# Gate logits taken from eight extra columns of two other products

## What is computed

```python
x = x + _L0_conv_ref(_gn(x), ...)          # linear attention on group-normed x
t = _to_tokens(x)
t = t + _L1_attn_ref(_ln_t(t), ...)        # softmax attention, 8 heads, + b_agg
t = t + _L1_ffn_ref(_ln_t(t), ...)         # routed experts
# inside the last:  gate_logits = ln(t) @ gate_weight   (256 x 8)
#                   gates = sinkhorn(max(logits, 1e-6)), 8 rounds; top 128 tokens for each of 8 experts
```

## Time and profile before

| what | us |
|---|---|
| median of 3 runs | 1494.82 (1491.95 to 1495.4) |
| span of the profiled execution, first to last instruction | 1467.7 |
| PE, PE weight load, DVE, ACT, POOL busy in it | 1339.3, 915.8, 1021.3, 868.7, 562.6 |
| mean granted TensorE clock, share of full speed | 0.950 |
| length of one ordinary attend (585 to 735 us, and so on) | 150 |

### The profile page before, as it was taken

One profiled execution on the slowest core, in us unless ns is written; L12 is line 12 of the kernel. 1 busy time (PEld: TensorE's weight loads), 2 busy tenths in 40 slices (PEclk: granted clock), 3 DMA queues, 4 the chain that ended last, 5 costly groups with the idle time before them and its releaser, 6 DMA issues.

```text
span 1467.7 us, 29142 instructions
## 1 busy us (share of the span) xinstructions
PE 1339.3 (91%) x10849; PEld 915.8 (62%) x10849; DVE 1021.3 (70%) x2114; ACT 868.7 (59%) x1268; POOL 562.6 (38%) x1068
## 2 busy tenths in 40 slices
PE   5789989999999999999999999999998999987535
PEld 3556656667576767676767676656666567766423
DVE  3536766858585857586768676787789776899771
ACT  2456557677667767677666767665675667542100
POOL 1132530445134513551245214520554116875443
PEclk9899989999999999999999999999999999999665
DMA  2051013600360037002710272005500265454322
GB/s 79 29 137 51 1 30 87 172 16 27 80 184 15 2 93 193 18 2 75 184 46 2 57 168 79 2 30 117 144 15 2 65 169 191 128 158 134 118 68 80
DMA packets 66785, 119.13 MB, mean 81 GB/s; under 512 B 10705, under 2 KB 46546, under 8 KB 66642
## 3 DMA queue, kind: packets, MB, share of 16 engines
q1 hardware_dynamic: 57682, 90.48, 22.9%
q0 software_dynamic: 8960, 26.75, 6.0%
HBM read 29.11 MB, written 33.55 MB: 43 GB/s over the span
## 4 chain that ended last, share of the span: by engine, by line
PE 62%; DVE 24%; issue 6%; POOL 4%; ACT 3%; DMA 0%; DVEq 0%; POOLq 0%; ACTq 0%
PE shared L938 30%; PE scores L894 12%; PE acc L916 11%; DVE prob_sum L1635 6%; PE acc L913 3%; PE shared L933 3%; DVE acc_sb L1609 2%; DVE bn L1344 2%; ACT probs L1209 2%; DVE work L1543 1%; PE acc L926 1%; DVE resid L1350 1%; DVE best_i L1541 1%; DVE best L1539 1%; DVE bn_x L1404 1%
## 5 line engine op out<-in xcount | busy, mean ns | idle before, releaser
L1209 ACT ACTIVATE probs<-scores 128x1024 f32<-128x1024 f32 x512 | 516.0, 1024 | 178.1 <-PE scores L894 94.0
L894 PE MATMUL scores<-query_stack,key_stack 96*128 96x256 f32 x2048 | 342.1, 308 | 16.0 <-ACT probs L1209 15.7
L1635 DVE TENSOR_TENSOR prob_sum<-prob_sum,probs 128x512 f32<-128x512 f32 x512 | 331.3, 707 | 0.0
L894 PEld LDWEIGHTS scores<-query_stack,key_stack 96*128 96x128 f32 x2048 | 275.9, 192 | 85.1 <-issue 39.1
L916 PE MATMUL acc<-probs,v_all 128*32 128x256 f32 x4096 | 289.2, 389 | 0.0
L1242 POOL TENSOR_TENSOR attn_T<-acc_sb 128x256 f32<-128x256 f32 x56 | 41.4, 740 | 447.8 <-DVE acc_sb L1609 445.0
L938 PE MATMUL shared<-w_sb,chan 128*128 128x512 f32 (+1 forms) x512 | 186.7, 501 | 5.9 <-DVE chan L1438 5.9
L916 PEld LDWEIGHTS acc<-probs,v_all 128*32 128x32 f32 x4096 | 114.8, 110 | 104.0 <-issue 37.9
L938 PEld LDWEIGHTS shared<-w_sb,chan 128*128 128x128 f32 x512 | 91.9, 192 | 62.5 <-issue 57.9
L938 PE MATMUL shared<-chan,w1T 128*128 128x512 f32 x256 | 121.3, 608 | 2.1 <-ACT chan L1125 2.1
L1635 DVE TENSOR_TENSOR prob_sum<-probs 128x512 f32<-128x512 f32 x128 | 98.4, 810 | 18.8 <-ACT probs L1209 16.5
(11 more groups left out here) (220 smaller groups left out, 2036.7 us busy)
## 6 DMA issues: line engine op xcount, KB each, us to landing
query_stack<-hi SPq DMA_DIRECT2D x120, 128.0 KB, 2.5
key_stack<-hi SPq DMA_DIRECT2D x120, 128.0 KB, 2.5
x_sb<-in_x_dram SPq DMA_DIRECT2D x8, 1024.0 KB, 5.3
out_dram<-resid SPq DMA_DIRECT2D x16, 512.0 KB, 4.8
tokens_scratch<-resid SPq DMA_DIRECT2D x16, 512.0 KB, 5.5
tokens_scratch<-rows SPq DMA_DIRECT2D x16, 512.0 KB, 3.3
key_stack<-lo SPq DMA_DIRECT2D x60, 128.0 KB, 2.5
query_stack<-lo SPq DMA_DIRECT2D x60, 128.0 KB, 2.5
```

Source lines behind the costliest of these rows:

```text
L894: last = pe.matmul(score_ps[u % 2][:, QB * r:QB * (r + 1)], key_stack[stack, HG * g + r, P * kt:P * (kt + 1)], query_stack[stack, HG * g + ...
L1209: act.activation(probs[:, u % PROBS, :], score_ps[u % 2][:, :], ACT.Exp, scale=DH ** -0.5) \
L1635: dve.tensor_tensor(total[:, part], probs[:, (u - 1) % PROBS, part] if kt == 1 else total[:, part], probs[:, u % PROBS, part], ALU.add).th ...
```

## The change

The logits are linear in the tokens up to the layer norm: with W the gate weights, logits = (t W - mean(t) sum(W)) / deviation(t). And t is the sum of what enters the attention and of the attention's output: t = lin_out + b_agg + attention w_agg. So the change takes `lin_out W` from the front, by 8 more columns in the `v` product (the rows that it multiplies are layer-normed, so ACT multiplies by the deviation and DVE adds the mean's share and that of the bias), and `attention w_agg W` from 8 more columns in the `agg` product. DVE adds the two, subtracts the mean's share, multiplies by the inverse deviation and clips.

Removed are the steps `z2T` and `gate`. Of their 16 places in the list two hold the new step `logits` (on DVE alone) and 14 a step `store_room` that issues nothing. `v` is eight steps of one tile, each weighted 0.9, where it was four of two tiles weighted 1.8. New are `deviations` and `means` (DVE alone, weight 0) around the `v` steps, and once in the first front `gate_weights` and `gate_sums`.

```diff
-             ("gvar",), ("store_stats", 1), ("z2T", 0), ("store_rows", 3), ("z2T", 1), ("z2T", 2), ("z2T", 3),
-             ("xn", 0), ("gate", 0), ("rest", 2), ("qk0", 0), ("gate", 1), ("store_rows", 4), ("qk0", 1), ("xn", 1),
...
+             ("gvar",), ("store_stats", 1), ("store_room", 0), ("store_rows", 3), ("store_room", 1), ("store_room", 2), ("store_room", 3),
+             ("xn", 0), ("store_room", 4), ("rest", 2), ("qk0", 0), ("store_room", 5), ("store_rows", 4), ("qk0", 1), ("xn", 1),
...
+    head[at:at] = [("weights_T", i) for i in range(2 * CH)] + [("bias",), ("gate_weights",), ("gate_sums",)]
...
# PE
-                    last = product(ps[:, 0:C], [(attn_T[:, c, tok[at[0]]], waggT[:, c, :]) for c in range(CH)])
-                elif kind == "z2T":
-                    pe.wait_ge(s["z2_ready"], T * seg.stores + at[0] + 1)
-                    last = transposes(ps, *(rows[:, at[0], half[c]] for c in range(CH)))
-                elif kind == "gate":
-                    last = product(ps[:, 0:E], [(z2T[:, c, tok[at[0]]], gate_w[:, c, :]) for c in range(CH)])
+                    last = product(ps[:, 0:C + E], [(attn_T[:, c, tok[at[0]]], waggT[:, c, :]) for c in range(CH)])
...
+                elif kind == "gate_weights":
+                    for c in range(CH):
+                        last = product(ps[:, E * c:E * (c + 1)],
+                                       [(env["wagg_nat"][:, o, half[c]], gate_w[:, o, 0:E]) for o in range(CH)])
+                elif kind == "gate_sums":
+                    pe.wait_ge(s["gate_bias_ready"], 1)
+                    last = product(ps[:, 0:2 * E], [(ones[:, :], gate_w[:, c, :]) for c in range(CH)])
...
+                    last = product(ps[:, 0:C + E], [(chan[:, c, tok[at[0]]], w1T[:, c, 2 * C:3 * C + E])
+                                                    for c in range(CH)])
# ACT
+                    act.activation(v_all[:, 0:G + 1:G, t, :], ps[:, 0:C].rearrange("p (g n) -> p g n", g=G), ACT.Copy)
+                    logits = gates[:, 0 if shifted_by_max else seg.front, t, :]
+                    read(act.activation(logits, ps[:, C:C + E], ACT.Copy, scale=ln_s[:, t:t + 1]), seg, *st)
# DVE
+                last = dve.tensor_tensor(target[:, t, :], ps[:, 0:C], source[:, t, :], ALU.add)
+                if kind == "agg":
+                    logits = logits_of(seg.store)[:, t, :]
+                    last = dve.tensor_tensor(logits, ps[:, C:C + E], logits, ALU.add)
...
+                elif kind == "logits":
+                    dve.wait_ge(s["row_r_ready"], stored + at[0] + 1)
+                    part = slice(T // 2 * at[0], T // 2 * (at[0] + 1))
+                    logits, means = logits_of(seg.store)[:, part, :], mean_part[:, part, :]
+                    link(means_times_sums(means, part))
+                    link(dve.tensor_tensor(logits, logits, means, ALU.subtract))
+                    link(dve.tensor_tensor(logits, logits, ln_r[:, part].unsqueeze(2).to_broadcast([P, T // 2, E]),
+                                           ALU.mult))
+                    dve.tensor_scalar(logits, logits, CLIP, None, ALU.max).then_inc(s["logits_ready"], 1)
...
+                elif kind == "deviations":
+                    dve.wait_ge(s["row_r_ready"], stored + 2 * seg.has("store") + 2)
+                    dve.tensor_tensor(ln_s[:, :], ln_v[:, :], ln_r[:, :], ALU.mult).then_inc(s["deviations_ready"], 1)
+                    link(means_times_sums(mean_part[:, :, :], slice(0, T)))
+                    link(dve.tensor_tensor(mean_part[:, :, :], mean_part[:, :, :],
+                                           gate_sums[:, E:2 * E].unsqueeze(1).to_broadcast([P, T, E]), ALU.add))
+                elif kind == "means":
+                    await_read(dve, seg, "v", T - 2)
+                    await_read(dve, seg, "v", T - 1)
+                    logits = logits_of(seg.front)
+                    link(dve.tensor_tensor(logits, logits, mean_part[:, :, :], ALU.add))
```

More of the change, by code:

```diff
@@ L86, in order @@
 def order(attend, front, store):
-    store_part = {"agg", "store_stats", "store_rows", "z2T", "gate"}
+    store_part = {"agg", "store_stats", "store_rows", "store_room", "logits"}
     attend_part = {"resid"}
@@ L118, in first_order @@
 def first_order():
-    steps = [x for x in order(False, True, False) if x[0] not in ("zT", "proj", "v", "square", "norms")]
+    steps = [x for x in order(False, True, False) if x[0] not in ("zT", "proj", "v", "deviations", "means", "square", "norms")]
     rows = [steps.index(("front_rows", t)) for t in range(T)]
@@ L179, in experts @@
         return steps + ([("expert", mine[-1]), ("put", mine[-1])] if behind else [])
-WORK = {"agg": 1.1, "store_stats": 0.5, "store_rows": 0.22, "z2T": 0.4, "gate": 0.4, "xT": 0.6, "x_stats": 0.4,
+WORK = {"agg": 1.1, "store_stats": 0.5, "store_rows": 0.22, "store_room": 0.4, "logits": 0.4, "xT": 0.6, "x_stats": 0.4,
         "gmean": 0.3, "gvar": 0.21, "xn": 0.8, "x_sum": 0.2, "resid": 0.0, "qk0": 1.8, "v0": 0.9,
         "head_stats": 0.28, "head_scale": 0.8, "sumv": 0.9, "dots": 3.5, "qT": 0.5, "lin": 1.1, "front_stats": 0.5,
-        "front_rows": 0.1, "zT": 0.9, "proj": 1.8, "v": 1.8, "square": 0, "copy_queries": 0, "center": 0, "weights_T": 0, "bias": 0, "norms": 0.5, "bound_rows": 0.5,
+        "front_rows": 0.1, "zT": 0.9, "proj": 1.8, "v": 0.9, "deviations": 0, "means": 0, "square": 0, "copy_queries": 0, "center": 0, "weights_T": 0, "bias": 0, "gate_weights": 0, "gate_sums": 0, "norms": 0.5, "bound_rows": 0.5,
         "bound": 0.3}
-BANKLESS = {"store_stats", "store_rows", "front_stats", "front_rows", "x_stats", "xn", "x_sum", "resid", "head_stats",
+BANKLESS = {"store_room", "logits", "deviations", "means", "store_stats", "store_rows", "front_stats", "front_rows", "x_stats", "xn", "x_sum", "resid", "head_stats",
             "head_scale", "square", "copy_queries", "center", "bound_rows", "col_scale", "row_sums", "row_scale", "top", "pick", "put"}
@@ L1384, in row_deviations, with logits_of, means_times_sums @@
                                          op1=ALU.mult).then_inc(s["row_r_ready"], 1)
+            def logits_of(b):
+                return gates[:, 0 if shifted_by_max else b, :, :]
+            def means_times_sums(out, part):
+                tiles = part.stop - part.start
+                return dve.tensor_tensor(out, mv[:, part, 0].unsqueeze(2).to_broadcast([P, tiles, E]),
+                                         gate_sums[:, 0:E].unsqueeze(1).to_broadcast([P, tiles, E]), ALU.mult)
             def step(seg, st):
@@ L1396, in step @@
                         row_deviations(at[0], stored + at[0])
-                elif kind == "gate":
-                    ps = await_full(dve, seg, *st)
-                    logits = logits_sb[:, E * at[0]:E * (at[0] + 1)] if shifted_by_max else gates[:, seg.store, at[0], :]
-                    read(dve.tensor_scalar(logits, ps[:, 0:E], CLIP, None, ALU.max), seg, *st)
+                elif kind == "logits":
[7 more added lines that the diff above has]
+                    dve.tensor_scalar(logits, logits, CLIP, None, ALU.max).then_inc(s["logits_ready"], 1)
+                elif kind == "gate_weights":
+                    await_small(dve)
+                    for c in range(CH):
+                        last = dve.tensor_scalar(gate_w[:, c, E:2 * E], gate_w[:, c, 0:E], bagg_T[:, c:c + 1], None,
+                                                 ALU.mult)
+                    last.then_inc(s["gate_bias_ready"], 1)
+                    ps = await_full(dve, seg, *st)
+                    read(dve.tensor_copy(waggT[:, :, C:C + E], ps[:, 0:CH * E].rearrange("p (c n) -> p c n", c=CH)),
+                         seg, *st)
+                elif kind == "gate_sums":
+                    ps = await_full(dve, seg, *st)
+                    read(dve.tensor_copy(gate_sums[:, :], ps[:, 0:2 * E]), seg, *st)
+                    await_read(dve, seg, *st)
+                elif kind == "deviations":
[9 more added lines that the diff above has]
+                    link(dve.tensor_tensor(logits, logits, mean_part[:, :, :], ALU.add))
```

97 lines of the change are left out of this document (50 added, 47 removed), and 3 rows, old and new, of the table steps.

## The result

The changed kernel's median is 1483.7 us (1475.47 to 1485.14, 4 runs), that of the kernel before 1495.11 (1491.95 to 1497.14, 4 runs): a ratio of 0.991, with a 95% interval of 0.9881 to 0.9938, or -11.4 us. Forecast were -7.2 us and 1487.6.

A forecast was written before the change was run, and what follows sets the result against it. PE and DVE were taken as level up to `gvar`, DVE a hair later, then POOL's chain beside PE, with PE leading after slot 8. Terms from start to tail sum to -7.2 us: 1494.8 to 1487.6, range 1470 to 1500.

The forecast's parts named there:

- start: First front: `gate_weights` and `gate_sums` delay DVE's head scaling, +2.2 us, with `v` +2.4; bounds 1 and 4.
- attend 0: First attend: only the front part of the change counts there, +0.3 us.
- attend 7: Last attend, with experts: part of its store's 5.1 us counts, early steps lie where DVE is full; -0.7 us.
- tail: After the attends: PE loses four `z2T` and four `gate`, but DVE carries this stage; -0.7 us.
- Ordinary attend: Attends 1 to 5: 0.9 us later at slot 8, 2.72 off by slot 11, `v` adds 0.24; net -1.5 each.
- about 0.9 later: Slot 8's scores end near 598.2 rather than 597.27 us, because DVE's additions delay `gvar` and POOL's chain.
- What would show it: Signs: PE near 145 us of 148.5, about 1 us wait before slot 8, DVE's chain 0.8 longer, `dots` at 56.4.
- The median lies 27.1 above the span: Whole kernel: the change touches nothing around the span, so the median goes from 1494.8 to 1487.6 us.
- A: PE is the bound throughout, no stalls form: 4.65 us off an attend, -26 in all, 1469; chance 0.20 including middle form.
- middle form: POOL's operations come out shorter, giving back perhaps 1.5 us an attend: 1479; shares the 0.20 chance of A.
- B: Gaps in PE's slots 4 to 8 cost the clock in attends 1 to 7: +14 us, 1502; chance 0.17.
- C: No measurable change: additions cost 1.5 us, imperfect hiding another 1.2 an attend; sum near 0, 1495; chance 0.21.

The follow-up runs named there:

- third trace of before: The kernel before, unchanged, profiled and timed again for a third trace: 1496.56 us, span 1494.6.
- the two second traces: The kernel before and the changed kernel, each unchanged and profiled once more: 1480.54 and 1484.23 us.
- on record: The execution of the kernel before that was profiled first, unchanged, on which the prediction was built: span 1467.7 us.
- the two early fills: Two dummy PE products per batch ahead of slot 8's scores, in the changed kernel and in that with `store_rows` 4 moved: 1480.38 and 1480.16 us.
- the later place: Changed kernel with `gate_weights` and `gate_sums` moved from behind `bias` to behind `proj` 1,0 in the first front: 1481.57 us, ratio 0.9917 to before.
- the kernel with both moves: Changed kernel with `store_rows` 4 behind slot 7's exponentials, `gate_weights` behind `dots` and `gate_sums` behind `lin` 1: 1465.35 us, ratio 0.9807 to before.
- the move: `store_rows` 4 put behind slot 7's exponentials: in the changed kernel 1472.05 us; in the kernel before, with `z2T` 4 following, ratio 0.997.

## Why the prediction was right, and where not

The sign, the mechanism and the order of size were right; that the sum comes near -7.2 is in part luck, for several terms are off in both directions. The third trace of before (time 1496.6) and that of after (1485.0) are both near their medians, and by the table above they differ thus:

| term | forecast | measured |
|---|---|---|
| start | +2.4 | +4.6 |
| attend 0 | +0.3 | +2.6 |
| attends 1 to 4 | -6.0 | -9.1 |
| attend 5 | -1.5 | -3.4 |
| attend 6 | -1.0 | -0.1 |
| attend 7 | -0.7 | -8.0 |
| tail | -0.7 | +2.2 |
| sum | -7.2 | -11.2 |

Without attend 7, the least certain term, -3.2 would be left. Between the two second traces (spans 1478.8 and 1482.7) the same table would end at +3.9, so no pair of traces shows the whole; that the change gained rests on the runs' ratio, 0.9881 to 0.9938, and on attends 1 to 4, which lost 9.0 to 9.4 us in every pair.

*Ordinary attend, -1.5 forecast, -2.25 measured.* Against the marks, from the block that ends the attend before (+0.28 us against before in the attend shown): `gvar` comes 0.57 later, not 0.8: an addition costs 0.07 and not the 0.1 that I took, and 8 x 0.07 = 0.56. POOL's chain keeps its length, as said. `store_rows` 4 is 0.44 later, the exponentials 0.45, the end of slot 8's scores (the start of `qk0` 2, 597.81 against 597.27) 0.26. The row of before, timeline of PE:
```profile
597.27 1.88 PE L938 MATMUL shared<-w_sb,chan 128*128 128x512 f32 x4
```
The step that failed is "about 0.9 later": the additions were priced at 0.8 for 0.56, and the slack of 0.38 us that I had read in the same rows wasn't taken off. 0.45 - 0.38 = 0.07 would have been left for the second unit's start; it is 0.12 later (597.23 against 596.83), and its end 0.26. From there to slot 12 it is -2.74, forecast -2.72. The `v` steps cost +0.24 at the block behind them, as priced. The sum, 0.26 - 2.74 + 0.24 = -2.24, is the attend's loss. On ACT an 8-column copy took 0.27 us, above my 0.1 to 0.2, and stayed hidden.

*What would show it.* Right: PE 145.5 us of 147.75; waits before slot 8 of 0.72 and 0.17; clock 1.00; DVE's pieces up to `gvar` broken, as before, by three gaps of half a microsecond alone. Wrong: DVE's stretch is 0.57 longer, not 0.8; ACT's wait before `store_rows` 4 is 1.76, not longer than 1.83, for ACT comes later too; `dots` starts at 57.8, not 56.4.

*Start.* The place was right, the price wrong: 12 records and two turns between the engines were to cost 2.2 us, and cost 3.7, because I took them at the clock of before. At half clock (0.50 from 51.2 to 53.1 us) the eight records alone took 1.88 us, and 1.87 or 1.88 in all seven traces; with the steps behind `dots` they took 0.96, at a clock of 1.00. The whole term, +4.6, lies above its upper bound of 4. The lower bound, that the products fall into gaps, is what that kernel reached.

*Attend 0* can't be read by itself: three traces of the kernel before give 157.6 to 163.0, with PE's clock down in different stretches. Taken with the start it can. Attend 1's first block has its mark at 275.3 to 281.2 us in the four traces with the first front of before, mean 278.8, and at 284.7 to 286.5 in the seven with that of the change, mean 285.8. The two terms, forecast at +2.7, came to +7.0. The sum had taken PE's clock as it was before. In the seven it was lower not only from 50 to 60 us but also from 70 to 80, 0.50 to 0.62 against 0.63 to 0.76; that this is the whole of the excess isn't shown.

*Tail, -0.7 forecast, +2.2 measured.* "PE is rid of four `z2T` and four `gate`, but DVE carries this stage" names the cause and then draws no cost from it. Timeline of DVE after:
```profile
1352.37 0.18 DVE L1405 TENSOR_TENSOR mean_part<-mv,gate_sums 128x32 f32<-128x32 f32 x1
...
1353.14 0.07 DVE L1595 MATCH_VALUE_LOAD work<-best,work 32x8 f32 x1
...
1372.25 0.16 DVE L1405 TENSOR_TENSOR mean_part<-mv,gate_sums 128x32 f32<-128x32 f32 x1
...
1373.00 0.07 DVE L1593 MATCH_VALUE_LOAD best_i<-best,work 32x8 f32 x1
```
The two `logits` steps stand among search operations without a gap: 0.77 + 0.75 us, and four additions 0.3, less some 0.5 for the clips. From the last block's copy to the last group's first column sum DVE needs 27.8 us; before it was 26.8 in the third trace, 26.1 on record and 23.1 in the second. Against the third, the trace of the table, this is 1.0 of the +2.2. The other 1.2 came behind it, and no experiment here was made for it.

*Attend 7, -0.7 forecast, -8.0 between these two traces.* This is the least certain term. Against the second trace of before it is -2.1, against the one on record +21.3. It holds the waits that the profile puts to nobody. Of the hand-overs on which they fell in the kernel before, ACT's copy of `z2T` (7.2 us in the third trace) and DVE's clip of `gate` (11.7) are gone, but `prob_sum` has 6.4 where it had none, ACT's `probs` 9.4 for 7.1, and `acc_sb` keeps 4.8 of 8.5. What these waits are, and whether the change shortens them, stays open; no experiment here was made for it.

*The time.* "The median lies 27.1 above the span; nothing in the change touches what is around it" was false in its first half: what lies around is 2 us, and 25 us were missing from that execution, whose attend 7 is 23 and 29 us shorter than in the two other traces. The forecast didn't suffer only because the difference, not the level, was worked out.

*The rivals.* A, PE the bound throughout, falls with the two early fills, and with it its middle form: POOL's chain kept its length. B falls in the ordinary attends: the largest new gap is 0.72 us and the clock stays 1.00. Its mechanism is real in the first front, where the clock is 0.52 from 50 to 60 us, behind a wait of PE of 2.66 us, and where it took back 2.8 of the 4 us that the later place had won. But behind the same wait the kernel with both moves has 0.83, so what decides it there is not settled. One reading behind B was wrong. The idle 1.05 us at 1152 is only what lies within the stretch of the earlier trace rows; the gap goes on past its end. Timeline of PE before at both places, and the stretch behind the second gap, columns as in the earlier trace rows:
```profile
1105.61 0.63 PE L933 MATMUL shared<-ident,lo 128*128 128x128 f32 x4 [1.41 <-POOL lo L787]
...
1154.37 0.66 PE L933 MATMUL shared<-ident,rows 128*128 128x128 f32 x4 [1.42 <-DVE lo L1494]
```
```profile
1154.00:1156.00 2.00, 1.63 (x21) 0.88 (x21) 2.00 (x5) 0.99 (x3) 0.00 (x0) 1.00 0.00 0
```
Both gaps are equally long. Behind the one the clock fell to 0.57, behind the other it stayed at 1.00 for the next 8 us, so "from a gap of between 1.05 and 1.41 us on" has no ground in these rows: the length of a single gap doesn't decide it. Beside B I had set the Trainium skill, "TensorE: Matmul & The Clock Gate", Part 1: the throttled clock is the default, and activity releases it. The first front with its waits agrees, at a clock of 0.52, and the gaps of up to 0.72 us in the ordinary attends show nothing of it, at 1.00. C falls with the attends' 2.25.

## What to carry to other kernels

An engine that is busy 99.5% of a stretch can still hide a second chain of the same length; look for the slack of that chain before counting removed work, and if there is none, move the step that waits. Here the change and the move were worth 2.25 and 0 us an ordinary attend alone, and 3.5 together. Before a level is built on a span, compare it with the executions' times: one profiled execution was 25 us below the median, and 11 below the quickest timed execution of the same kernel. And before a rule is drawn from idle time in a stretch, look up the gap itself in the timeline: it may go on past the stretch.

## What the runs showed that was not expected

ACT and DVE stood together with nobody on the core named, up to 9.6 us at a time and 38 to 60 us in all, the longest time while POOL issued gathers, in twelve of thirteen traces; attend 7 is 18 to 29 us longer in them than in the one without, which issues the same gathers. The same eight small products cost PE 1.88 us at one place of the first front and 0.96 at another, at clocks of 0.50 and 1.00, and one order of steps cost 2 us in the 56 products behind it. Moving one step of ACT by one slot took 4.7 to 6.5 us off attend 6, for a reason that stays open.
